# Rows' low half with an operand in PSUM, row stores and one tile moved in the queues, x rows loaded first, last group stored in pieces

## The chip, the cores and the metric

The kernel runs as one program on one core of a Trainium2 chip. The metric is the device time of one execution in microseconds (us), the median of three runs. TensorE (PE), VectorE (DVE), ScalarE (ACT) and GpSimd (POOL) each work through a list of instructions of their own, in order, and wait for each other on semaphores. SyncE (SP) only issues transfers; they run beside the engines on one hardware queue (q1) that 16 DMA engines serve.

## What is computed

The input x and the context have shape (8, 512, 2048), fp32. The reference, cut to what matters:

```python
# 1. autocorrelation attention, 8 heads of 256 columns, per batch
q = layernorm(x); k = v = context
corr = ifft(fft(q) * conj(fft(k))).real            # along the 512 positions
w, idx = top_k(corr, 12); w = softmax(w)           # per batch, head and column
out = sum_i w_i * v[min(idx_i + pos, 511)]
x = x + out
# 2. a linear layer with 16 low-rank updates, on h = layernorm(x)
x = x + h @ W.T + bias + sum_e ((h @ A_e.T) @ Bf_e.T) * (coeffs * scales)_e
```

## The kernel before

The work is written as one pipeline of 78 windows (`for w in range(windows + 1)`, the same loop on each engine's list); a window handles several jobs at once, each at its own delay.

**Attention.** One chunk is one batch and one head: 512 positions by 256 columns. Chunk n has its correlation and its top 12 in window n, its output in window n + 1; there are 64. The transforms are fp32 matmuls with constant matrices, among them `fold` (used first by `values(0)`), which PE can't start without. On POOL, `fold_values` and `fold_queries` add and subtract halves of the operands, `add_products`, `add_upper` and `add_lower` combine products (the helper `add`, line 1042). On DVE, `multiply_queries`, `multiply_upper` and `multiply_lower` multiply PSUM by SBUF (`product`, line 1167). The second half of `multiply_lower` (its tiles a_tw and a_tf) waits until POOL has done the `add_products` of the next window.

**Preparation of the weights, windows 0 to 9.** The 16 row tiles of the combined weight matrix (W plus the low-rank updates) are each made by PE (`delta`, into the PSUM tensor f_ps), added on DVE (`tile_add`), scaled and split into a fp16 high half on ACT (`tile_high`) and a fp16 low half on POOL (`tile_low(n)`, line 1135: p_lo = p_w - p_hi), transposed by DMA (`turn_high`, `turn_low`) and stored to DRAM (`store_high`, `store_low`). Two tiles are done per window. In windows 2 to 9 POOL does `tile_low(2w-4)` after its attention work and `tile_low(2w-3)` at the window's end. So the last tile, number 15, has its low half made at the end of window 9, just ahead of the `add_products` of window 10.

**Rows, from window 9 on.** Row tile r (128 rows, 2048 columns) of batch b is handled in window 9 + 8b + (r mod 4). POOL adds the attention to x (`add_row`), SP stores the sum (`store_x1`), DVE finds the statistics (`row_statistics`, `row_gain`), ACT normalises in place once the store has landed (`row_normalise`, line 959) and writes the fp16 high half row_hi (`row_high`). In the next window, after `multiply_lower`, DVE makes the low half:

```python
def row_low(w, r):
    dve.wait_ge(hi_done, r + 1)
    at_least(dve, h_out, 32 * r)
    nc.vector.tensor_tensor(row_lo[:, :], rows[w % 2][:, :], row_hi[:, :], ALU.subtract).then_inc(lo_done, 1)
```

This is line 1308, tile f_rowlo. Both of its inputs are in SBUF. SP then stores both halves (`store_h`). In window 13 (`LAG - 1`) SP waits until all weights are out, and loads the first weights, and the four row tiles of batch 0 by a transposing DMA (`load_h`, line 516).

**Linear layer, from window 14 on.** Each window runs half of the product of one batch with one group of 512 output columns: 96 fp16 matmuls between the attention's matmuls (high times high, high times low, low times high; lines 781, 783, 785), into f_ps. From there DVE scales (`scale_group`), POOL adds to x1p (`add_group`, 128x512 at a time, four times), and SP stores 1 MB (`store_group`, line 535). There are 32 groups. f_ps is thus free between window 8 and window 14.

**The start.** SP issues chunk 0 of the context (vs) and its last row (last, broadcast to all partitions), the matrix `fold`, four row tiles of x of 1 MB each (`load_first_rows`, line 573, into a_rows and p_w), then chunk 0 of x (xs). DVE finds the first batch's statistics from the four row tiles (`first_statistics`, `first_gain`). ACT's list begins with `double_last(0)`, `move_values(0)`, `move_upper(0)`, which copy PE's results on the context, and only then comes `normalise(0)` (line 875), which needs those statistics. After it POOL begins `fold_queries(0)`.

**Order on SP.** SP's list decides when transfers start, since a wait in it holds back all that stands behind. In window 9 it has `turn_high(14)`, `load_rows`, then the transposes and stores of tile 14 and `turn_high(15)`, and behind them `store_x1(9, 0)` and the load of the next attention rows.

Of the kernel before, what the change touches and what calls it, by code (L numbers as in the profile page):

```python
# [30 lines left out]
ALU = mybir.AluOpType  # L31
# [3 lines left out]
T = 128  # L35
BATCH, L, D = 8, 512, 2048
TB = L // T
# [65 lines left out]
def at_least(engine, sem, value):  # L103

    if isinstance(value, int) and value <= 0:
        return
    engine.wait_ge(sem, value)
# [106 lines left out]
def flow(nc, shared, x, W, A, Bf, coeffs, scales, parts, x1s, hrow, bias, whi, wlo, wscale, out):  # L214
# [12 lines left out]
    with ExitStack() as ctx:  # L227
# [168 lines left out]
        f_shift_done = sem("f_shift_done")  # L396
        h_done = sem("f_h_done")
        hi_done = sem("f_hi_done")
        lo_done = sem("f_lo_done")
        product_mm = sem("f_product_mm")  # L400
        y_done = sem("f_y_done")
# [37 lines left out]
        def _(sp):  # L439
# [23 lines left out]
            def load_attn(r, early):  # L463

                if r >= TILES:
                    return
                at_least(sp, row_added, r)
                if r == 0 and early:
                    sp.wait_ge(delta_mm, TB * OT)
                cols = slice(0, D) if r % TB else slice(0, D - CH) if early else slice(D - CH, D)  # L470
                sp.wait_ge(parts_out, 16 * (CHUNKS * (r // TB + 1) - (r % TB == 0 and early)))
                sp.dma_start(attn[:, cols], part_rows[r * T:(r + 1) * T, cols]).then_inc(attn_in, 16)
# [5 lines left out]
            def store_x1(w, r):  # L478
                sp.wait_ge(row_added, r + 1)
                sp.dma_start(x1s[r * T:(r + 1) * T, :], rows[w % 2][:, :]).then_inc(x1_out, 16)  # L480
# [27 lines left out]
            def load_h(b, q):  # L508

                if b >= BATCH:  # L510
                    return
                unit_read(16 * (b - 1) + 12 + q)
                sp.wait_ge(h_out, 32 * TB * (b + 1))
                cols = slice(q * KQ * T, (q + 1) * KQ * T)
                for dst, part in ((h_hi, 0), (h_lo, 1)):
                    sp.dma_start_transpose(dst[q][:, :, :], hrow[part, b * L:(b + 1) * L, cols]).then_inc(h_in[q], 16)  # L516
# [14 lines left out]

            def store_group(g):
                b, cols = g // 4, slice(g % 4 * WC, (g % 4 + 1) * WC)
                sp.wait_ge(y_added, TB * (g + 1))
                sp.dma_start(out[b, :, cols].rearrange("(i p) d -> p i d", p=T), x1p[:, :, :]).then_inc(out_out, 16)

# [17 lines left out]
            def turn_low(n):  # L554
                sp.wait_ge(p_lo_done, n + 1)
                at_least(sp, p_lo_out, 16 * n)
                sp.dma_start_transpose(p_lo_t[:, :, :], p_lo[n % 2][:, :]).then_inc(p_lo_turned, 16)
# [4 lines left out]
            def store_high(n):  # L562
                sp.wait_ge(p_hi_turned, 16 * (n + 1))
                sp.dma_start(tile_of(whi, n), p_hi_t[n % 2][:, :, :].rearrange("p (q k) o -> p q (k o)", k=KQ)
                             ).then_inc(p_hi_out, 16)

            def store_low(n):
                sp.wait_ge(p_lo_turned, 16 * (n + 1))
                sp.dma_start(tile_of(wlo, n), p_lo_t[:, :, :].rearrange("p (q k) o -> p q (k o)", k=KQ)
                             ).then_inc(p_lo_out, 16)  # L570

            def load_first_rows(k, dst):
                sp.dma_start(dst, x_rows[k * T:(k + 1) * T, :]).then_inc(px_in[k], 16)

            shared.load_v(sp, 0)
            shared.load_fold(sp)
            load_first_rows(0, rows[0][:, :])
            load_first_rows(1, rows[1][:, :])
            load_first_rows(2, w_sb[:, 0, :])
            load_first_rows(3, w_sb[:, 1, :])  # L580
            shared.load_x(sp, 0)
            shared.load_matrices(sp)
            sp.dma_start(ident, shared.consts["ident"]).then_inc(shared.ident_in, 16)
            shared.load_v(sp, 1)
# [15 lines left out]
            for w in range(windows + 1):  # L600
                r, g, at = row_tile(w), finished_group(w), product_window(w)
                made = 1 < w <= PREPARED + 1
                unit = 2 * (w - LAG)
                if 0 < w <= PREPARED:
                    load_rows(w + 1)
                load_x(w + 3)
                if r is not None and r % TB == 0:
                    load_attn(r, False)
                if made:
                    turn_high(2 * w - 4)  # L610
                if at:
                    load_weights(unit + 2)
                if g is not None:
                    store_group(g)
                    load_group(g + 1)
                if row_tile(w - 1) is not None:
                    store_h(row_tile(w - 1))
                if w > PREPARED:
                    load_rows(w + 1)
                if at and at[1] == 7:  # L620
                    for q in range(2):
                        load_h(at[0] + 1, q)
                if made:
                    store_high(2 * w - 4)
                    turn_low(2 * w - 4)
                    load_tile(2 * w - 4 + PW)
                    turn_high(2 * w - 3)
                    store_low(2 * w - 4)
                if r is not None:
                    store_x1(w, r)  # L630
                    if r % TB < TB - 1:
                        load_attn(r + 1, True)
                if w == LAG - 1:
                    sp.wait_ge(p_hi_out, 16 * OT)
                    sp.wait_ge(p_lo_out, 16 * OT)
                    sp.wait_ge(scale_out, 16 * OT)
                    load_weights(0)
                    load_weights(1)
                    load_group(0)
                if at:  # L640
                    load_weights(unit + 3)
                load_v(w + 3)
                if w == LAG - 1:
                    for q in range(4):
                        load_h(0, q)
                if at and at[1] == 7:
                    load_h(at[0] + 1, 2)
                if made:
                    store_high(2 * w - 3)
                    turn_low(2 * w - 3)  # L650
                    load_tile(2 * w - 3 + PW)
                    store_low(2 * w - 3)
                if PREPARED + 1 <= w < PREPARED + 1 + TB:
                    for n in range(TB * (w - PREPARED - 1), TB * (w - PREPARED)):
                        sp.dma_start(wscale[n * T:(n + 1) * T].unsqueeze(1), down[:, n:n + 1]).then_inc(scale_out, 16)
                if 1 <= w <= N:
                    store_parts(w - 1)
                if w >= CHUNKS and w % CHUNKS == 0 and w // CHUNKS <= BATCH:
                    load_attn(TB * (w // CHUNKS - 1), True)
                if at and at[1] == 7:  # L660
                    load_h(at[0] + 1, 3)
            sp.wait_ge(out_out, 16 * 4 * BATCH)

        @block.tensor
        def _(pe):
# [197 lines left out]
        def _(act):  # L863
            def copy(out, source, **how):
                return nc.scalar.activation(out, source, ACT.Copy, **how)  # L865
# [96 lines left out]
            def row_high(w, r):  # L962
                act.wait_ge(h_done, r + 1)
                at_least(act, h_out, 32 * r)
                copy(row_hi[:, :], rows[w % 2][:, :]).then_inc(hi_done, 1)

            def tile_sums(w, n):

# [68 lines left out]
        def _(pool):  # L1037
# [105 lines left out]
            for w in range(windows + 1):  # L1143
                r, g, at = row_tile(w), finished_group(w), product_window(w)
                if 0 < w < N:
                    add_products(w)
                if g is not None:
                    add_group(g)
                if 1 <= w <= N:
                    add_upper(w - 1)  # L1150
                if 1 <= w <= N:
                    add_lower(w - 1)
                if r is not None:
                    add_row(w, r)
                if 1 < w <= PREPARED + 1:
                    tile_low(2 * w - 4)
                fold_queries(w + 2)
                fold_values(w + 2)
                if 1 < w <= PREPARED + 1:
                    tile_low(2 * w - 3)  # L1160
                if at and at[1] % 2 == 1:
                    add_bias(4 * at[0] + at[1] // 2)

        @block.vector
        def _(dve):
# [139 lines left out]
            def row_low(w, r):  # L1305
                dve.wait_ge(hi_done, r + 1)
                at_least(dve, h_out, 32 * r)
                nc.vector.tensor_tensor(row_lo[:, :], rows[w % 2][:, :], row_hi[:, :], ALU.subtract).then_inc(lo_done, 1)  # L1308

            def scale_group(g):  # L1310

# [146 lines left out]
```

## Time and profile before

| | |
|---|---|
| median of 3 runs | 2785.59 us (2785.28 to 2786.66) |
| the profiled execution's own time | 2788.0 us |
| its span, first to last instruction | 2786.0 us |
| PE busy | 2647.7 us, 95% |
| POOL busy | 2165.1 us, 78% |
| DVE busy | 1839.6 us, 66% |
| ACT busy | 1097.0 us, 39% |
| granted TensorE clock, mean | 0.979 |

The profile is of one execution. The engines' busy times overlap. A row of the timeline gives the start, the duration, engine, line and tiles of an instruction (or of several merged ones, x2, x4), and in brackets how long the engine sat idle before it and for what. The chain of waits is followed back from the last instruction; what isn't on it had room. SPq is SP's queue issuing transfers. All rows on which the prediction rests are listed below, in groups.

### The profile page before, as it was taken

The numbers are of one execution on the slowest core, as the hardware profiler recorded it, in microseconds if no ns is written. First come the engines' busy times: TensorE is split into PE (matmuls) and PEld (weight loads), VectorE is DVE, ScalarE is ACT, GpSimd is POOL, SyncE is SP. The second block draws the span as 40 slices with busy tenths as digits, with TensorE's granted clock in tenths as the row PEclk, the third lists the DMA queues.
The fourth block names the chain that finished last, engine by engine and source line by source line (L and its number), as shares of the span: only waits on it lengthen the run. The fifth ranks groups of instructions, "written<-read, shape, count | busy, mean of one in ns | idle before, by whom it ended". The sixth has DMA issues, their size and how long they took to land.

```text
span 2786.0 us, 39716 instructions
## 1 busy us (share of the span) xinstructions
PE 2647.7 (95%) x14112; PEld 1706.3 (61%) x14112; DVE 1839.6 (66%) x4710; ACT 1097.0 (39%) x1873; POOL 2165.1 (78%) x1558
## 2 busy tenths in 40 slices
PE   5999855899999999999999999999999999999998
PEld 4666644566666666666666666666666666664443
DVE  5888889766776677666776677667766577644200
ACT  4777734533343343433444344443433244211000
POOL 5899988777897799877897799877897789645222
PEclk8999978899999999999999999999999999999999
DMA  8499985845676566945776476845775476548953
GB/s 311 113 267 263 247 233 130 239 145 203 234 235 207 192 225 224 262 138 189 248 236 211 174 245 221 248 154 186 249 207 166 168 246 225 165 147 303 293 171 113
DMA packets 444390, 587.30 MB, mean 211 GB/s; under 512 B 216992, under 2 KB 343072, under 8 KB 426528
## 3 DMA queue, kind: packets, MB, share of 16 engines
q1 hardware_dynamic: 444192, 584.76, 66.1%
q8 instruction: 112, 1.84, 0.3%
q14 instruction: 86, 0.70, 0.1%
HBM read 383.35 MB, written 151.00 MB: 192 GB/s over the span
## 4 chain that ended last, share of the span: by engine, by line
PE 79%; POOL 6%; DMA 5%; DVE 5%; SPq 2%; issue 2%; ACT 1%; POOLq 0%; DVEq 0%; ACTq 0%
PE f_ps L781 14%; PE f_ps L785 14%; PE f_ps L783 14%; PE a_ps L710 10%; PE a_ps L668 10%; PE a_ps L746 7%; PE a_ps L761 3%; PE a_ps L762 3%; PE a_ps L723 2%; DVE f_rowlo L1308 2%; POOL p_lo L1135 1%; DMA p_hi_t<-p_hi 1%; SPq L516 1%; DMA out_dram<-f_x1p 1%; DMA x_scratch<-a_rows 1%
## 5 line engine op out<-in xcount | busy, mean ns | idle before, releaser
L781 PE MATMUL f_ps<-f_whi,f_hhi 128*128 128x512 f16 x2048 | 776.9, 379 | 3.9 <-DMA f_hlo<-h_scratch 2.4
L785 PE MATMUL f_ps<-f_whi,f_hlo 128*128 128x512 f16 x2048 | 776.9, 379 | 0.0
L783 PE MATMUL f_ps<-f_wlo,f_hhi 128*128 128x512 f16 x2048 | 776.7, 379 | 0.0
L865 ACT ACTIVATE a_side<-a_ps 128x256 f32<-128x256 f32 (+1 forms) x192 | 87.1, 454 | 961.4 <-PE a_ps L746 726.9
L710 PE MATMUL a_ps<-a_w_lag,lags 128*128 128x256 f16 x3072 | 356.2, 273 | 1.3 <-DVE a_tf L1167 1.3
L785 PEld LDWEIGHTS f_ps<-f_whi,f_hlo 128*128 128x128 f16 x2048 | 200.5, 98 | 242.1 <-issue 0.8
L783 PEld LDWEIGHTS f_ps<-f_wlo,f_hhi 128*128 128x128 f16 x2048 | 200.5, 98 | 224.8 <-issue 0.8
L710 PEld LDWEIGHTS a_ps<-a_w_lag,lags 128*128 128x128 f16 x3072 | 300.2, 98 | 60.2 <-issue 4.6
L781 PEld LDWEIGHTS f_ps<-f_whi,f_hhi 128*128 128x128 f16 x2048 | 200.5, 98 | 212.5 <-issue 5.0
L1042 POOL TENSOR_TENSOR a_prod<-a_prod,a_tf 128x512 f32<-128x512 f32 x128 | 160.5, 1275 | 215.5 <-DVE a_tf L1167 215.5
L1042 POOL TENSOR_TENSOR a_zv<-a_zv,a_tw 128x512 f32<-128x512 f32 x128 | 187.1, 1480 | 132.8 <-DVE a_tf L1167 132.7
L746 PE MATMUL a_ps<-inv,a_prod 128*128 128x256 f32 x1024 | 238.8, 387 | 23.4 <-POOL a_prod L1042 23.4
L1042 POOL TENSOR_TENSOR f_x1p<-f_x1p,f_y 128x512 f32<-128x512 f32 x128 | 160.5, 1287 | 102.5 <-DVE f_y L1167 102.5
L746 PEld LDWEIGHTS a_ps<-inv,a_prod 128*128 128x128 f32 x1024 | 198.1, 194 | 62.3 <-POOL a_prod L1042 28.6
L1167 DVE TENSOR_TENSOR f_y<-f_ps,f_scale 128x512 f32<-128x512 f32 x128 | 81.1, 686 | 198.9 <-PE f_ps L785 171.7
L1042 POOL TENSOR_TENSOR f_x1p<-f_x1p,f_bias 128x2048 f32<-128x2048 f32 x32 | 147.3, 4602 | 70.4 <-DMA f_x1p<-x_scratch 70.4
L668 PE MATMUL a_ps<-a_tv,fold 128*128 128x256 f32 x512 | 133.6, 408 | 54.9 <-ACT a_vk L865 54.9
L1042 POOL TENSOR_TENSOR a_zu<-a_zu,a_tu 128x512 f32<-128x512 f32 x128 | 172.4, 1369 | 4.2 <-DVE a_tu L1167 4.2
L1214 DVE TENSOR_TENSOR a_ps<-a_ps,a_side 128x256 f32<-128x256 f32 x128 | 55.2, 431 | 181.0 <-ACT a_side L865 181.0
L865 ACT ACTIVATE a_w_lag<-a_ps 128x1024 f16<-128x1024 f16 x128 | 124.0, 1020 | 128.2 <-PE a_ps L723 128.2
L1042 POOL TENSOR_TENSOR a_rows<-a_rows,f_attn 128x2048 f32<-128x2048 f32 x32 | 144.2, 4507 | 33.8 <-DMA f_attn<-parts_scratch 33.8
L1167 DVE TENSOR_TENSOR a_prod<-a_ps,a_vk 128x512 f32<-128x512 f32 x128 | 87.9, 687 | 122.3 <-PE a_ps L668 122.3
(130 smaller groups left out, 5324.8 us busy)
## 6 DMA issues: line engine op xcount, KB each, us to landing
f_whi<-whi_scratch SPq DMA_DIRECT2D x128, 512.0 KB, 5.4
f_wlo<-wlo_scratch SPq DMA_DIRECT2D x128, 512.0 KB, 6.6
a_rows<-in_x_dram SPq DMA_DIRECT2D x62, 1024.0 KB, 8.4
vs<-in_ctx_dram SPq DMA_DIRECT2D x64, 512.0 KB, 7.6
xs<-in_x_dram SPq DMA_DIRECT2D x64, 512.0 KB, 3.6
parts_scratch<-a_so SPq DMA_DIRECT2D x64, 512.0 KB, 4.7
x_scratch<-a_rows SPq DMA_DIRECT2D x32, 1024.0 KB, 5.1
f_x1p<-x_scratch SPq DMA_DIRECT2D x32, 1024.0 KB, 6.2
```

What stands on the lines that cost most here:

```text
L668: return nc.tensor.matmul(ps[:, pair, j, :], fold[:, k, :], source, start=True, stop=True)
L710: mm = nc.tensor.matmul(ps[:, pair + k, cls, :], lag_mat[:, constant, j, 2 * cls + k, :], w_lag[:, part, 2 * h + j::TB, :], start=(j == 0 ...
L723: mm = nc.tensor.transpose(turned[:, i * T:(i + 1) * T], w_row[:, part, i // TB, i % TB * T:(i % TB + 1) * T], shared.ident16[:, :])
L746: mm = nc.tensor.matmul(corr[:, g, cls * 2 * T:(cls + 1) * 2 * T], prod[:, 2 * k + cls, g * T:(g + 1) * T], inv[:, cls, k, :], start=(k == ...
L761: nc.tensor.matmul(ps[:, 2 + j, i, :], outm[:, k0, :], z[:, s0, :], start=True, stop=False)
L762: mm = nc.tensor.matmul(ps[:, 2 + j, i, :], outm[:, k1, :], z[:, s1, :], start=False, stop=True)
L781: nc.tensor.matmul(f_ps[:, t, :], h_hi[q][:, kq, rows_t], w_hi[u % WR][:, :, kq, :], start=(k == 0), stop=False)
L783: nc.tensor.matmul(f_ps[:, t, :], h_hi[q][:, kq, rows_t], w_lo[u % WR][:, :, kq, :], start=False, stop=False)
L785: mm = nc.tensor.matmul(f_ps[:, t, :], h_lo[q][:, kq, rows_t], w_hi[u % WR][:, :, kq, :], start=False, stop=(k == DB - 1))
L865: return nc.scalar.activation(out, source, ACT.Copy, **how)
L1042: return nc.gpsimd.tensor_tensor(whole, whole, part, op)
L1167: return nc.vector.tensor_tensor(out, a, b, ALU.mult)
```

## The change

Four edits, and nothing else:

1. For the first four rows (r < 4), ACT copies row_hi once more, as fp32 into the PSUM tensor f_ps, and DVE subtracts that copy instead of row_hi. The result is the same number.
2. On SP, `store_x1` and the load of the next attention rows stand ahead of the tile's transposes and stores. Both are in one window only in window 9.
3. The low half of tile 15 and its transpose and store are taken from window 9 to window 10. On POOL it comes after `add_row` and before `fold_queries`.
4. At the start the first two row tiles of x come first, and `fold` after chunk 0 of x. At the end the last group is stored in four pieces of 256 KB, each after its own addition.

```diff
             def store_group(g):
                 b, cols = g // 4, slice(g % 4 * WC, (g % 4 + 1) * WC)
+                if g == 4 * BATCH - 1:
+                    for t in range(TB):
+                        sp.wait_ge(y_added, TB * g + t + 1)
+                        sp.dma_start(out[b, t * T:(t + 1) * T, cols], x1p[:, t, :]).then_inc(out_out, 16)
+                    return
...
-            shared.load_v(sp, 0)
-            shared.load_fold(sp)
             load_first_rows(0, rows[0][:, :])
             load_first_rows(1, rows[1][:, :])
+            shared.load_v(sp, 0)
             load_first_rows(2, w_sb[:, 0, :])
             load_first_rows(3, w_sb[:, 1, :])
             shared.load_x(sp, 0)
+            shared.load_fold(sp)
...
+                if r is not None:
+                    store_x1(w, r)
+                    if r % TB < TB - 1:
+                        load_attn(r + 1, True)
                 if made:
                     store_high(2 * w - 4)
                     turn_low(2 * w - 4)
                     load_tile(2 * w - 4 + PW)
                     turn_high(2 * w - 3)
                     store_low(2 * w - 4)
-                if r is not None:
-                    store_x1(w, r)
-                    if r % TB < TB - 1:
-                        load_attn(r + 1, True)
...
                 if made:
                     store_high(2 * w - 3)
+                if 1 < w <= PREPARED:
                     turn_low(2 * w - 3)
                     load_tile(2 * w - 3 + PW)
                     store_low(2 * w - 3)
+                if w == PREPARED + 2:
+                    turn_low(OT - 1)
+                    store_low(OT - 1)
...
                 copy(row_hi[:, :], rows[w % 2][:, :]).then_inc(hi_done, 1)
+                if r < TB:
+                    act.wait_ge(hi_done, r + 1)
+                    at_least(act, lo_done, r)
+                    copy(f_ps[:, :, :].rearrange("p a c -> p (a c)"), row_hi[:, :]).then_inc(hi_copied, 1)
...
                 if r is not None:
                     add_row(w, r)
+                if w == PREPARED + 2:
+                    tile_low(OT - 1)
                 if 1 < w <= PREPARED + 1:
                     tile_low(2 * w - 4)
                 fold_queries(w + 2)
                 fold_values(w + 2)
-                if 1 < w <= PREPARED + 1:
+                if 1 < w <= PREPARED:
                     tile_low(2 * w - 3)
...
-                nc.vector.tensor_tensor(row_lo[:, :], rows[w % 2][:, :], row_hi[:, :], ALU.subtract).then_inc(lo_done, 1)
+                high = row_hi[:, :]
+                if r < TB:
+                    dve.wait_ge(hi_copied, r + 1)
+                    high = f_ps[:, :, :].rearrange("p a c -> p (a c)")
+                nc.vector.tensor_tensor(row_lo[:, :], rows[w % 2][:, :], high, ALU.subtract).then_inc(lo_done, 1)
```

## Rows read from the trace of the kernel before

**Rows 1.** Windows: length, busy time of each engine, granted clock, DMA share, GB/s.
```profile
385.50:403.20 17.70, 5.89 (x20) 4.54 (x18) 17.70 (x3) 0.77 (x2) 17.62 (x12) 0.69 0.75 119
625.20:2455.00 1829.80, 1829.80 (x10152) 1204.05 (x10152) 1268.91 (x3290) 713.34 (x1293) 1532.41 (x1118) 1.00 0.64 209
```
**Rows 2.** Timeline of DVE, windows 9 to 13: two waits for POOL, and the four row_low.
```profile
383.09 1.29 DVE L1167 TENSOR_TENSOR a_tw<-a_ps,a_vk 128x512 f32<-128x512 f32 x2 [7.87 <-POOL a_prod L1042]
385.49 17.68 DVE L1308 TENSOR_TENSOR f_rowlo<-a_rows,f_rowhi 128x2048 f16<-128x2048 f32 x1
432.28 2.28 DVE L1308 TENSOR_TENSOR f_rowlo<-a_rows,f_rowhi 128x2048 f16<-128x2048 f32 x1
446.98 2.47 DVE L1290 BATCH_NORM_STATS2 f_bn<-a_rows 128x6 f32<-128x512 f32 x4 [0.79 <-POOL a_rows L1042]
463.48 17.69 DVE L1308 TENSOR_TENSOR f_rowlo<-a_rows,f_rowhi 128x2048 f16<-128x2048 f32 x1
510.52 2.28 DVE L1308 TENSOR_TENSOR f_rowlo<-a_rows,f_rowhi 128x2048 f16<-128x2048 f32 x1
```
**Rows 3.** Chain of waits, windows 9 to 14: start, length, what.
```profile
385.58 17.60 DVE f_rowlo L1308
...
535.28 0.38 PE f_ps L781
```
**Rows 4.** Timeline of POOL over the same windows.
```profile
364.94 1.27 POOL L1071 TENSOR_TENSOR a_tq<-xs 128x512 f32<-128x512 f32 x1
376.47 4.07 POOL L1135 TENSOR_TENSOR p_lo<-p_w,p_hi 128x2048 f16<-128x2048 f32 x1
380.50 2.49 POOL L1042 TENSOR_TENSOR a_prod<-a_prod,a_tf 128x512 f32<-128x512 f32 x2
398.55 1.25 POOL L1071 TENSOR_TENSOR a_tq<-xs 128x512 f32<-128x512 f32 x1
401.10 3.20 POOL L1076 TENSOR_TENSOR xs<-a_tq 128x512 f32<-128x512 f32 x1
425.27 2.52 POOL L1042 TENSOR_TENSOR a_prod<-a_prod,a_tf 128x512 f32<-128x512 f32 x2 [6.84 <-DVE a_tf L1167]
432.44 4.46 POOL L1042 TENSOR_TENSOR a_zv<-a_zv,a_tw 128x512 f32<-128x512 f32 x2 [1.51 <-DVE a_tf L1167]
458.47 2.50 POOL L1042 TENSOR_TENSOR a_prod<-a_prod,a_tf 128x512 f32<-128x512 f32 x2
```
**Rows 5.** DVE groups with an input in PSUM: durations in ns, least, median, most.
```profile
L1256 DVE SCALAR_TENSOR_TENSOR a_w_row<-a_ps,a_sums,a_w_row x128: 740/747/753, 55.4 to 2469.7; 128x512 f16<-128x512 f32 x128
L1167 DVE TENSOR_TENSOR a_zv<-a_ps,a_vk x128: 680/681/692, 69.9 to 2483.6; 128x512 f32<-128x512 f32 x128
L1343 DVE TENSOR_SCALAR p_bt<-f_ps,p_mix x2: 3685/3688/3690, 38.0 to 56.7; 128x2048 f32<-128x2048 f32 x2
```
**Rows 6.** Timeline of ACT around the row work of windows 9 and 10.
```profile
378.11 2.09 ACT L959 ACTIVATE a_rows<-a_rows,f_shift,f_gain 128x2048 f32<-128x2048 f32 x1 [12.51 <-DMA x_scratch<-a_rows]
424.90 1.91 ACT L865 ACTIVATE f_rowhi<-a_rows 128x2048 f16<-128x2048 f32 x1
```
**Rows 7.** Timeline of the start: PE, ACT, the issue of chunk 0 of x.
```profile
4.45 0.64 SPq L179 DMA_DIRECT2D xs<-in_x_dram  x1
14.24 3.75 PE L668 MATMUL a_ps<-vs,fold 128*128 128x256 f32 x8 [14.24 <-POOL vs L1062]
21.34 0.62 ACT L865 ACTIVATE a_uk<-a_ps 128x256 f32<-128x256 f32 x2
23.90 2.07 ACT L875 ACTIVATE xs<-xs,stat 128x256 f32<-128x256 f32 x4 [1.94 <-DVE stat L1336]
```
**Rows 8.** Time to landing of that transfer of chunk 0 of x.
```profile
DMA to landing us min/median/max: 14.7/14.7/14.7
```
**Rows 9.** The last store: its issue in the timeline, its bytes in a window.
```profile
2781.45 0.39 SPq L535 DMA_DIRECT2D out_dram<-f_x1p  x1
2784.00:2785.00 1.00, 0.00 (x0) 0.00 (x0) 0.00 (x0) 0.00 (x0) 0.00 (x0) 0.50 1.02 377
```

More of the change, by code:

```diff
@@ L398, in flow @@
         hi_done = sem("f_hi_done")
+        hi_copied = sem("f_hi_copied")
         lo_done = sem("f_lo_done")
@@ L661, in _ @@
                     load_h(at[0] + 1, 3)
-            sp.wait_ge(out_out, 16 * 4 * BATCH)
+            sp.wait_ge(out_out, 16 * (4 * BATCH - 1 + TB))
         @block.tensor
```

## The prediction

> **What bounds the kernel now.** I read the windows first. From 625 to 2455 us PE is busy for 1829.8 of 1829.8 us at the full clock [rows 1]: in the steady part nothing but PE's own work counts, and the change takes none of it away. What can move is what lies before the first product (it starts at 535.28 [rows 3], when the first transposed low half has landed) and what lies after the last. So I read the chain of waits before 535 next. Its two longest pieces by far are one and the same DVE instruction, the subtraction of line 1308, with 17.60 us each; the first stands in [rows 3]. The timeline shows that the same instruction on the same shape takes 2.28 us in the windows between [rows 2]. Over the first of the two, POOL is busy for 17.62 of 17.70 us, and PE and ACT nearly idle [rows 1]. The held instruction ends at 403.2, and in the last 2 us of it POOL's instruction at 401.10 is stretched to 3.20 us, where its like before it takes 1.25 [rows 4]: DVE gets in there, and holds POOL in turn. In the two short cases it is POOL that had just been waiting 1.5 us for DVE's a_tf, so DVE comes first, and POOL's next pair is stretched [rows 4]. So this is DVE shut out by a row of POOL instructions, when both of its inputs are in SBUF. Before that, window 9 has 7.87 us in which DVE waits for POOL's a_prod, behind tile 15's low half [rows 2, 4].
>
> **Edit 1, the operand in PSUM.** DVE's instructions with one input in PSUM and one in SBUF show no such case: 128 of line 1167 between 680 and 692 ns, 128 of line 1256, with an fp16 input and output, between 740 and 753 ns, in all windows and beside the same POOL work [rows 5]. So I take the hold as gone. The new instruction's own length isn't in the trace. Its ends are 2.28 us (the SBUF form [rows 2]) and 3.69 us (the 2048 columns of line 1343 out of the same f_ps, written with a stride [rows 5]); I take 2.4, since four 512-column products at 0.6 us from start to start come to that, and they are its nearest kin. Each hold is 17.69 - 2.28 = 15.4 us.
>
> ACT gets one copy more per row, 1.91 us by its twin [rows 6], at most 2.1 by line 959 [rows 6]; into PSUM it could be a little shorter, below which I have no row. In window 10 row_hi was done at 424.90 + 1.91 = 426.8, and DVE wanted it at 432.28 [rows 2, 6]: 5.5 us of room for a copy of 1.9, so the new wait costs nothing. Behind it stand `normalise` of a later chunk, which POOL needs a window later, and in window 13 the statistics and `part_corr`: about 1 us there, hidden under the wait for the transposed rows. Were that cover gone, it would be 1 us once.
>
> The Trainium skill (SBUF — State Buffer, "Who interferes with whom") says that a DVE instruction with two SBUF inputs contends with a GpSimd instruction that reads SBUF, and one with at most one SBUF input doesn't; the rows on PSUM inputs agree. Its section "SBUF: two separate sides" has whoever starts first hold the ports for one whole instruction. By that the held DVE would wait for one POOL instruction, 4.5 us at most, and the gain would be 9 us for two, not 31; here the row shows 15.4 us over eleven POOL instructions, and I go by the row.
>
> **Edits 2 and 3, windows 9 and 10.** Without tile 15's 4.07 us, a_prod of window 10 starts at 376.5, not 380.5 [rows 4], and DVE's a_tw 4.0 earlier, at 379.1. ACT doesn't stand in the way: its row_normalise waited 12.51 us for the row's store [rows 6], which SP issued behind the transposes; with the store ahead of them it lands around 366, and row_hi and its copy are done by 374.5. The transposes and stores of tiles 14 and 15 come later on SP by two issues, about 1 us, and nobody waits for them before window 13. So the first row_low starts at 381.5 and ends at 383.9, where before it ended at 403.2: 19.3 us. What DVE does next needs the correlation, which begins with the same a_prod and moves by 4.0 only; it may cost DVE 1 us of this.
>
> In window 10 POOL is now late. From a_prod (380.50) to the first a_tq (398.55) it took 18.05 us, and from a_tq to the next a_prod 11.53 (364.94 to 376.47) [rows 4]. With tile 15 between them: 376.5 + 18.05 + 4.05 + 11.53 = 410.1, a_prod done at 412.6, while DVE would be ready at about 411. So the second row_low starts at 412.7 + 2.4 = 415.1, not 432.28: 17.2 us gained. This is where the moved tile costs its 4 us, of which about 2.4 are covered by DVE's longer window.
>
> From there each window is DVE's: the free one lasted 31.20 us from row_low to row_low (432.28 to 463.48 [rows 2]). Of these 0.79 went on a wait for POOL's row sum [rows 2], which POOL, no longer stretched and waiting (1.51 + 1.96 us at 432.44 [rows 4]), now has ready; plus 0.2 for the longer subtraction: 30.6. POOL's own round is 18.05 + 11.53 = 29.6, just below. So the third starts at 445.7 (before: 463.48) and the fourth at 476.3 (before: 510.52), 34.2 earlier, and ends 34.0 earlier. What follows to the first product, 22.5 us of SP issues and transfers, stays. PE is ready for it with about 2 us of room. Gain by edits 1 to 3: 34.0 us. The ends: 37 if the windows fall to POOL's 29.6, 27 if each subtraction takes 3.69 and POOL holds windows at 33.2 (425.27 to 458.47 [rows 4]).
>
> **Edit 4, start and end.** Up to chunk 0 of x, eight transfers are issued, and in the change the same eight, with `fold` the last instead of chunk 0 of x. The last of the eight landed at 4.45 + 14.7 = 19.1 [rows 7, 8]; so `fold` lands then. PE's first matmul, at 14.24 before [rows 7], needs it: 4.9 us later. ACT copies PE's results before it may normalise; these copies ended at 22.0 [rows 7], now at 26.9, and the statistics, 0.6 earlier than before (256 KB less ahead of the rows), wait for ACT. So normalise(0) starts at 26.9, not 23.90 [rows 7]: 3.0 us lost, and the chain runs from it through POOL without room. The bounds: a gain of 0.6 if `fold` comes in time after all, a loss of 5.
>
> At the end 1 MB is issued at 2781.45, moves at 377 GB/s [rows 9], 2.7 us, and the span ends at 2786.0. Now 256 KB remain after the last addition, 0.7 us: 1.9 us gained (0 to 2.7: the transfer's fixed part stays). The three earlier issues lie under POOL's additions.
>
> The Trainium skill (DMA: Bandwidth & Descriptors, "HWDGE ordering") has descriptors consumed in ring order on each DMA engine. If several transfers shared the bandwidth instead, `fold` would be in before the rows and the start would cost nothing.
>
> **Sum.** -34.0 + 3.0 - 1.9 = -32.9 us. The profiled execution took 2788.0 us, 2.0 more than its span and 2.4 more than the median. So 2755.1 for such an execution, and 2785.6 - 32.9 = 2752.7 for the median.
>
> **Rivals.** (a) POOL becomes the bound between windows 10 and 13: its round is 29.6 against DVE's 30.6, so little is wanting. At 33.2 us a window, and the long form of the subtraction, 27 instead of 34: 2760. For it: its round has hardly a pause. Against: part of the 33.2 was the stretching by row_low. (b) Only one of the two holds goes, or both by half, as they would if the lock were passed on at each instruction: 15.4 less, 2768; by the page's lock rule it is 2775. Against: two holds of the same 17.6. (c) The change doesn't do what it says: the copy in PSUM doesn't free DVE. Then row 0 waits as before for POOL's pause, which the moved tile puts at the same moment, and what remains is +3.0 - 1.9: 2787. (d) Slower: the PSUM form is held as well, and POOL, now less often behind DVE, is in full run at rows 1 and 3 too, which were let through only thanks to its 1.5 us of waiting. Place: row_low of windows 11 and 13; price 15.4 each; one of them is enough: 2787 + 15.4 = 2802. Rows 5 speak against (c) and (d): 256 cases without one.
>
> **Chances.** Forecast 0.78, (a) 0.10, (b) 0.05, (c) 0.04, (d) 0.03. The range 2745 to 2766 takes the forecast with its bounds and (a). This kernel can be told from no change at about 0.2%, 5.6 us. Faster 0.93 (forecast, a, b), same 0.04 (c), slower 0.03 (d).
>
> **What would show it.** Right: f_rowlo at 2.3 to 2.5 us in all four rows; the first product near 504; a_tw's wait for a_prod in window 9 down from 7.9 to about 3.9 us; PE's first matmul at about 19 and ACT's normalise at about 27; some 2 us less between the last addition and the end; the rest of the same length. Wrong: any f_rowlo of the first four over 5 us; ACT as the last releaser of row_low; a product start later than 512.

## The result, and the profile after

Four runs of the changed kernel had a median of 2753.39 us (2749.87 to 2755.55), four of the kernel before beside them 2785.44 us (2783.86 to 2786.66): a ratio of 0.9881, 95% interval 0.9866 to 0.9896. Forecast were 2752.7 us. The profiled execution took 2753.61 us against 2788.0, which is 34.4 us less; the sum had said 32.9.

The page after, its span, the busy times and the shares of the chain by engine:
```profile
span 2751.5 us, 39727 instructions
PE 2642.9 (96%) x14112; PEld 1702.8 (62%) x14112; DVE 1811.5 (66%) x4710; ACT 1103.7 (40%) x1877; POOL 2157.1 (78%) x1558
PE 81%; POOL 6%; DMA 5%; DVE 4%; SPq 2%; issue 2%; ACT 1%; POOLq 0%; DVEq 0%; ACTq 0%
```
The first four row_low are one group now, and ACT has four copies more. The groups by form (duration in ns least, median, most; first to last start; the shapes):
```profile
L1328 DVE TENSOR_TENSOR f_rowlo<-a_rows,f_ps x4: 2274/2277/2278, 381.9 to 477.5; 128x2048 f16<-128x2048 f32 x4
L875 ACT ACTIVATE f_ps<-f_rowhi x4: 1882/1882/1882, 373.7 to 472.1; 128x2048 f32<-128x2048 f16 x4
```
Where two of the four took 17.7 us [rows 2], all four take 2.28. The timeline of DVE in windows 9 to 13, the lines that answer to [rows 2]:
```profile
379.52 1.29 DVE L1183 TENSOR_TENSOR a_tw<-a_ps,a_vk 128x512 f32<-128x512 f32 x2 [2.66 <-POOL a_prod L1056]
381.92 2.28 DVE L1328 TENSOR_TENSOR f_rowlo<-a_rows,f_ps 128x2048 f16<-128x2048 f32 x1
413.19 1.29 DVE L1183 TENSOR_TENSOR a_tw<-a_ps,a_vk 128x512 f32<-128x512 f32 x2 [2.34 <-POOL a_prod L1056]
415.59 2.28 DVE L1328 TENSOR_TENSOR f_rowlo<-a_rows,f_ps 128x2048 f16<-128x2048 f32 x1
419.61 0.43 DVE L1230 TENSOR_TENSOR a_ps<-a_ps,a_side 128x256 f32<-128x256 f32 x1 [1.07 <-ACT a_side L875]
447.44 2.27 DVE L1328 TENSOR_TENSOR f_rowlo<-a_rows,f_ps 128x2048 f16<-128x2048 f32 x1
477.51 2.28 DVE L1328 TENSOR_TENSOR f_rowlo<-a_rows,f_ps 128x2048 f16<-128x2048 f32 x1
```
The wait for a_prod ahead of the first is down from 7.87 to 2.66 us; there is now a short wait for POOL in the next window as well (2.34). The same stretch on POOL, where [rows 4] has its lines of before:
```profile
376.93 2.49 POOL L1056 TENSOR_TENSOR a_prod<-a_prod,a_tf 128x512 f32<-128x512 f32 x2
...
382.51 2.49 POOL L1056 TENSOR_TENSOR a_zv<-a_zv,a_tw 128x512 f32<-128x512 f32 x2
...
395.01 4.06 POOL L1149 TENSOR_TENSOR p_lo<-p_w,p_hi 128x2048 f16<-128x2048 f32 x1
...
401.61 1.27 POOL L1090 TENSOR_TENSOR xs<-a_tq 128x512 f32<-128x512 f32 x1
...
410.59 2.49 POOL L1056 TENSOR_TENSOR a_prod<-a_prod,a_tf 128x512 f32<-128x512 f32 x2
```
Nothing of POOL is stretched in these windows any more: the pair of additions at 382.51, beside the first row_low, takes 2.49 us, where [rows 4] shows 4.46 for such a pair, and the instruction at 401.61 takes 1.27, where [rows 4] shows 3.20 for its like. DVE and POOL run past each other. Tile 15 stands where it was moved to, at 395.01.

The first product, from the timeline of PE:
```profile
502.26 0.38 PE L791 MATMUL f_ps<-f_whi,f_hhi 128*128 128x512 f16 x1 [1.57 <-DMA f_hlo<-h_scratch]
```
It stood at 535.28 [rows 3], so 33.0 us come from ahead of it. From there to the start of DVE's four products of the last group (`scale_group`) it is 2240.1 us before and 2240.4 after. That they agree so closely says little: over the ten traces of this document this stretch lies between 2237.8 (the second trace of the changed kernel) and 2240.5, with no order by kernel, so it is unchanged within some 2.7 us. From those products to the end of POOL's last addition it is 6.05 us in both. From there to the end of the span 4.6 us have become 2.8. 33.0 - 0.3 + 1.8 = 34.5, which is the whole difference of the spans.

### The profile page after: what moved, and what is told of

Its sections match the earlier page's. It is cut to its first block, busy times and chain, and to the rows that moved or that the text cites. A ratio compares the mean times of both kernels' runs of the same rounds, so it can differ in the third digit from the quotient of the medians.

```text
span 2751.5 us, 39727 instructions
## 1 busy us (share of the span) xinstructions
PE 2642.9 (96%) x14112; PEld 1702.8 (62%) x14112; DVE 1811.5 (66%) x4710; ACT 1103.7 (40%) x1877; POOL 2157.1 (78%) x1558
## 4 chain that ended last, share of the span: by engine, by line
PE 81%; POOL 6%; DMA 5%; DVE 4%; SPq 2%; issue 2%; ACT 1%; POOLq 0%; DVEq 0%; ACTq 0%
PE f_ps L791 15%; PE f_ps L793 15%; PE f_ps L795 15%; PE a_ps L678 10%; PE a_ps L720 10%; PE a_ps L756 7%; PE a_ps L771 3%; PE a_ps L772 3%; PE a_ps L733 2%; POOL p_lo L1149 1%; SPq L517 1%; PE f_ps L817 1%; DMA out_dram<-f_x1p 1%; DMA x_scratch<-a_rows 1%; DMA p_hi_t<-p_hi 1%
## 5 line engine op out<-in xcount | busy, mean ns | idle before, releaser
L1056 POOL TENSOR_TENSOR a_zf<-a_zf,a_tf 128x512 f32<-128x512 f32 x128 | 159.4, 1264 | 0.0
```

The lines of the kernel that those rows point to most:

```text
L1056: return nc.gpsimd.tensor_tensor(whole, whole, part, op)
```

## The experiments

Two sets, each on one chip beside the kernel before: the first four rows of the table (there the kernel before had a median of 2786.52 us), and the last four (2786.99 us). "Row_low" gives the start of the four, with the length where it isn't 2.28 us.

| kernel | median us | ratio, 95% interval | row_low of rows 0 to 3, us | first product |
|---|---|---|---|---|
| edit 1 alone | 2754.3 | 0.9889, 0.9874 to 0.9903 | 383.3, 414.0, 445.3, 475.3 | 500.39 |
| edits 2 and 3 alone | 2787.7 | 1.0002, 0.9993 to 1.0011 | 382.6 (21.7), 432.0, 463.2 (17.7), 510.2 | 535.93 |
| all, operand in SBUF | 2787.6 | 1.0004, 0.9994 to 1.0013 | 379.8 (21.7), 431.1, 462.5 (17.5), 509.6 | 534.86 |
| PSUM for rows 0 and 2 | 2768.3 | 0.9943, 0.9927 to 0.9960 | 384.8, 418.4 (17.7), 463.8, 493.9 | 518.75 |
| the change again | 2754.4 | 0.9884, 0.9869 to 0.9898 | 381.4, 415.1, 445.8, 477.1 | 502.19 |
| old start | 2752.3 | 0.9873, 0.9858 to 0.9887 | 380.0, 413.6, 446.1, 477.4 | 503.19 |
| before, with one wait | 2758.5 | 0.9896, 0.9882 to 0.9911 | 385.9 (2.8), 417.6 (2.8), 449.2 (2.8), 481.6 | 507.48 |
| with two moves more | 2747.4 | 0.9860, 0.9843 to 0.9876 | 377.9, 409.7, 439.7, 471.1 | 496.66 |

**Edit 1 alone.** The kernel before with this, and nothing moved:
```diff
+                if r < TB:
+                    act.wait_ge(hi_done, r + 1)
+                    at_least(act, lo_done, r)
+                    copy(f_ps[:, :, :].rearrange("p a c -> p (a c)"), row_hi[:, :]).then_inc(hi_copied, 1)
...
+                    high = f_ps[:, :, :].rearrange("p a c -> p (a c)")
+                nc.vector.tensor_tensor(row_lo[:, :], rows[w % 2][:, :], high, ALU.subtract).then_inc(lo_done, 1)
```


> Edit 1 alone on the kernel before. Theory (two SBUF inputs let POOL shut DVE out): f_rowlo of the first four rows at 2.3 us each, the first product near 503.5 (535.3 less 31.7: window 9 keeps its 4 us of tile 15, window 10 loses nothing to it), no gain at the end: 2756 in the profiled execution, about 2754 median, ratio 0.9886. Rival (the queue edits carry a good part): at most half of the gain, 2770 or more.

Its timeline of DVE:
```profile
380.86 1.29 DVE L1172 TENSOR_TENSOR a_tw<-a_ps,a_vk 128x512 f32<-128x512 f32 x2 [6.39 <-POOL a_prod L1047]
383.26 2.28 DVE L1317 TENSOR_TENSOR f_rowlo<-a_rows,f_ps 128x2048 f16<-128x2048 f32 x1
...
475.32 2.29 DVE L1317 TENSOR_TENSOR f_rowlo<-a_rows,f_ps 128x2048 f16<-128x2048 f32 x1
```
Its ratio can't be told from that of the whole change: edit 1 is the gain. What edits 2 and 3 add is seen when the times are counted from one point that both kernels pass alike, the low half of tile 13 in window 8. From there to the four row_low it is 47.4, 78.1, 109.4 and 139.4 us here, and 43.7, 77.3, 109.2 and 139.2 in the change: a start 3.7 us ahead at the first, of which 0.8 is left at the second and 0.2 at the fourth. Tile 15's 4 us of POOL only went from window 9 to window 10.

**Edits 2 and 3 alone**, with row_low out of SBUF:

> Edits 2 and 3 alone, row_low with two SBUF inputs. Theory: the first row_low starts 4 us earlier and is still held until POOL's first pause, which the tile moved into window 10 keeps at about 403; from there all is as before: 2788 +-1.5, ratio 1.000. Rival (the queue edits give their 4 us for themselves): 2784 or less. Second rival (POOL in full run holds rows 1 or 3 as well): 2803 or more.

DVE's row 0, then POOL's list beside it:
```profile
382.60 21.68 DVE L1315 TENSOR_TENSOR f_rowlo<-a_rows,f_rowhi 128x2048 f16<-128x2048 f32 x1
```
```profile
395.65 4.04 POOL L1140 TENSOR_TENSOR p_lo<-p_w,p_hi 128x2048 f16<-128x2048 f32 x1
...
402.21 3.20 POOL L1081 TENSOR_TENSOR xs<-a_tq 128x512 f32<-128x512 f32 x1
```
The subtraction is 4.0 us longer than 17.68 [rows 2], which is the length of the one instruction put into POOL's list. So the hold lasts as long as the list, and by itself the move brings nothing that the times show.

**All of the change, the operand in SBUF.** The copy, its wait and its place stay; DVE reads the other operand:
```diff
                 high = row_hi[:, :]
                 if r < TB:
                     dve.wait_ge(hi_copied, r + 1)
-                    high = f_ps[:, :, :].rearrange("p a c -> p (a c)")
```


> The changed kernel, with the copy into PSUM and the wait for it kept, but DVE subtracting row_hi from SBUF. Theory: rows 0 and 2 are held 15 us or more each, row 1 is let through; first product near 535, 2786.5 profiled, ratio 1.000. Rival (it is the later start or the order of waits that frees DVE, not the operand): f_rowlo near 2.3 us, 2753.6, ratio 0.988.

DVE's timeline of it, row 0:
```profile
379.82 21.66 DVE L1327 TENSOR_TENSOR f_rowlo<-a_rows,f_rowhi 128x2048 f16<-128x2048 f32 x1
```
This differs from the change in one operand only and loses all of it. So neither ACT's copy nor the wait for it, which shifts when DVE asks, makes the gain; the operand does. It differs in two ways, though: it lies in SBUF and is fp16, where the copy lies in PSUM and is fp32. No run has an fp32 copy in SBUF. That the memory decides and not the type is argued: line 1256 reads an fp16 operand in SBUF beside one in PSUM and was never held [rows 5], so an fp16 operand alone doesn't make the hold; but no held or free instruction with two fp32 inputs in SBUF was measured.

**PSUM for rows 0 and 2 only**, the two that were held before. Here the theory and rival (d) differ: is a row that was let through still let through when POOL no longer waits ahead of it?
```diff
-                if r < TB:
+                if r in (0, 2):
```


> The changed kernel with the PSUM operand for rows 0 and 2 only; rows 1 and 3 subtract from SBUF. Theory (what decides is whether POOL is in full run when DVE asks): in the changed kernel row 1 asks at 415.6, between two POOL instructions without a pause until 431; so row 1 is held, 15 to 16 us, and row 3, which asks while POOL waits for DVE's a_tf, is not: one window more, 2768 profiled, ratio 0.994. Rival (the holds belong to rows 0 and 2, by their buffer or place): no f_rowlo over 3 us, 2753.6, ratio 0.988.

DVE's row 1, and POOL from before it asks until it is let in:
```profile
418.38 17.67 DVE L1328 TENSOR_TENSOR f_rowlo<-a_rows,f_rowhi 128x2048 f16<-128x2048 f32 x1
```
```profile
418.30 0.71 POOL L1056 TENSOR_TENSOR a_zu<-a_zu,last 1x256 f32<-1x256 f32 x1
...
432.64 1.25 POOL L1086 TENSOR_TENSOR a_tq<-xs 128x512 f32<-128x512 f32 x1
433.97 3.20 POOL L1090 TENSOR_TENSOR xs<-a_tq 128x512 f32<-128x512 f32 x1
...
494.02 4.46 POOL L1056 TENSOR_TENSOR a_zv<-a_zv,a_tw 128x512 f32<-128x512 f32 x2 [0.38 <-DVE a_tf L1183]
```
Row 1, free in the kernel before, is held for 17.67 us here, and half of the gain is gone. Row 3 is free again: POOL had waited 0.38 us just before. So which rows are held isn't a matter of the row but of whether POOL's list has a pause when DVE asks. That part of rival (d) is real; it doesn't touch the change because all four rows read PSUM.

Where DVE is let in can be read from the code: the stretched instruction is the same in each held row (401.10 [rows 4], 402.21 and 433.97 above), and it is the one ahead of which `fold_queries` waits for POOL's own instruction just before (`pool.wait_ge(q_halved, n + 1)`). The next run puts a wait of this kind where DVE asks.

**One wait for POOL.** The kernel before, in which POOL waits ahead of the additions into a_zv for its own addition just before:
```diff
                 pool.wait_ge(w0_used, 2 * (n + 1))
+                pool.wait_ge(zu_raised, n + 1)
                 add(zv[:, 0:2, :], tw[:, 0:2, :], ALU.add)
```


> The kernel before with one wait more on POOL: ahead of add_lower's first addition it waits for its own last instruction, so that its list has a pause just where DVE asks for row_low. Nothing else. Theory (DVE gets in at POOL's first pause, however short): f_rowlo of rows 0 and 2 at about 3 us instead of 17.7, each window loses 2.3 us of POOL in turn, first product near 507, 2759.5 profiled, ratio 0.990. Rival (a pause of this kind is too short, or DVE waits its turn over a number of instructions): still 15 us or more for rows 0 and 2, ratio 1.000.

DVE's row 0, and POOL beside it:
```profile
385.89 2.78 DVE L1309 TENSOR_TENSOR f_rowlo<-a_rows,f_rowhi 128x2048 f16<-128x2048 f32 x1
```
```profile
385.80 0.71 POOL L1042 TENSOR_TENSOR a_zu<-a_zu,last 1x256 f32<-1x256 f32 x1
386.65 4.37 POOL L1042 TENSOR_TENSOR a_zv<-a_zv,a_tw 128x512 f32<-128x512 f32 x2
```
Both operands are in SBUF, and the row takes 2.78 us. POOL stood still from 386.51 to 386.65; that 0.14 us is enough to let DVE in. The price is on POOL: its pair takes 4.37 us, not 2.49, 1.9 in each window with a row_low. From tile 13's low half the first row_low comes after 47.4 us, as with edit 1 alone, and the fourth after 143.1, which is 3.7 more; POOL lost three times 1.9 in between, of which 2.0 don't show in DVE's times. In the whole time this kernel and edit 1 alone can't be told apart by their intervals.

**The change again, with old start, and with two moves more.** "Old start" has the loads of the start in their old order and is otherwise the change. The last kernel has the old start too; the low half of tile 15 is made by DVE in window 9, out of a copy in PSUM as the rows are; and of the last group, the third and fourth row tile are multiplied and added by DVE, with the product left in PSUM:
```diff
+                    dve.wait_ge(last_copied, 1)
+                    nc.vector.tensor_tensor(p_lo[(OT - 1) % 2][:, :], w_sb[:, (OT - 1) % PW, :],
+                                            f_ps[:, :, :].rearrange("p a c -> p (a c)"), ALU.subtract
+                                            ).then_inc(last_low, 1)
...
+                    if g == 4 * BATCH - 1 and t >= 2:
+                        product(f_ps[:, t, :], f_ps[:, t, :], scale_sb[:, :]).then_inc(y_in_ps, 1)
+                        nc.vector.tensor_tensor(x1p[:, t, :], x1p[:, t, :], f_ps[:, t, :], ALU.add
+                                                ).then_inc(half_added, 1)
```


> The changed kernel once more, on the same chip as the three that follow, as what they are compared with: ratio 0.988, about 2753.

> The changed kernel with the start's transfers in the old order. Theory of the prediction (fold last costs the start): PE's first matmul back at 14.2 and ACT's normalise at 23.9 instead of 25.5, and if nothing takes it up on the way, 1.6 us off the whole, 2751.8. What the two traces suggest instead: the transfer-paced windows 3 to 8 swallow it (the delay was 1.55 us at POOL's first fold_queries and 0.3 us at tile 13's low half in window 8), so the whole stays within 1 us of the changed kernel.

> A version meant to beat both: the changed kernel with the old start, tile 15's low half made on DVE in window 9 with its high half in PSUM (instead of on POOL in window 10), and in the last group the additions of the third and fourth row tile on DVE, out of PSUM. Theory: DVE's wait for a_prod in window 10 (2.34 us) goes, the last addition ends 2 us sooner; 2749 profiled, ratio 0.9865. Rival (transfers or ACT take it back): no better than the changed kernel, 0.988.

With the old start ACT's first `normalise` begins at 23.58 us, with the new one at 25.47 and 26.15. The whole is 2.1 us shorter, but the intervals overlap. Tile 13's low half, ahead of which all kernels do the same but for the start, begins between 334.4 and 339.3 us in six traces with the old start, the kernel before among them, and between 336.3 and 341.3 in four with the new. The means are 1.4 us apart, within spreads of 5. There is one more comparison: the kernel with the operand in SBUF has the new start and the last store in pieces, the one with edits 2 and 3 alone has neither (nor ACT's copies). The last store in pieces is worth 1.8 us, yet their medians, of ten runs each on one chip, differ by 0.2 (2787.6 and 2787.7), which leaves 1.6 for the new start. None of these is clear of the spread by itself; all of them point to a cost of 1.4 to 2.1 us, where the expectation for the old start's run had leaned to under 1. So the new start probably costs something, but that isn't shown.

DVE's timeline of the last kernel:
```profile
343.38 2.28 DVE L1433 TENSOR_TENSOR p_lo<-p_w,f_ps 128x2048 f16<-128x2048 f32 x1
...
407.25 1.28 DVE L1195 TENSOR_TENSOR a_tw<-a_ps,a_vk 128x512 f32<-128x512 f32 x2
...
2740.48 0.69 DVE L1352 TENSOR_TENSOR f_x1p<-f_x1p,f_ps 128x512 f32<-128x512 f32 x1
```
The tile takes DVE 2.28 us instead of POOL's 4.06, and the wait of 2.34 us ahead of a_tw is gone. From tile 13's low half to the fourth row_low it is 136.7 us, where the change has 139.2 in both of its traces and the kernel with the old start, which does the same there, 140.9: 2.5 to 4.2 gained. At the end, from DVE's first product of the last group to the end of the span, 8.8 us have become 7.6. It is the shortest of all kernels here: 0.9860 of the kernel before; against the change's 0.9884 the intervals overlap a little.

## Why the prediction was right

**The hold and its end.** Taken: two holds of 15.4 us, gone with the operand in PSUM. Measured: all four at 2.28 us, and with row_hi in SBUF as the operand the loss of everything. The mechanism is as stated, and stronger than stated: the hold follows POOL's list to the instruction (17.7 us; 21.7 with 4.04 more in the list; 2.8 with a pause of 0.14). The rule in the Trainium skill (SBUF — State Buffer, "SBUF: two separate sides"), that whoever starts first keeps the ports for one whole instruction, gives a wait of less than 5 us here. The runs show eleven instructions of POOL in a row, twelve with the tile, and the measurement decides. The same page's "Who interferes with whom", that a DVE instruction with at most one SBUF input doesn't contend, agrees with all runs here. One reading of the prediction was loose: over the first hold PE was busy for 5.89 of 17.70 us [rows 1], which isn't "nearly idle"; nothing was worked out from it.

**Length of the new subtraction.** Taken 2.4 us, between 2.28 and 3.69; it is 2.28, the length of the SBUF form. The ACT copy, taken at 1.91, is 1.88, and it was never what row_low waited for.

**Windows 9 and 10.** The wait for a_prod was to fall to 3.9 us; it is 2.66 in one trace and 3.71 in the second (there at 379.03), so the forecast holds about as well as two executions agree. The second row_low was foretold at 415.1 and measured at 415.59; POOL's a_prod done at 412.6, measured 413.08. That is where POOL is late, and the moved tile costs there what the step said: of the lead of 3.7 us at the first row, which edits 2 and 3 gave, 0.8 is left at the second.

**The free windows.** Taken 30.6 us each; measured 31.85 and 30.07, and 30.74 and 31.26 in the second trace. They follow from one number: a window lasts 30.1 us, and what DVE waits for ACT's copies of PE's results comes on top. In the 31.85 these are two waits, 1.07 us for the correlation's odd half (419.61, above) and 0.65 for the output's; in the 30.07 there is none; in the second trace 0.69 (30.74) and 1.12 (31.26). This stretch of PE, first its timeline, then the window's totals (busy time by engine, granted clock, DMA share, GB/s), shows what was late ahead of the first of the two:
```profile
413.14 6.02 PE L756 MATMUL a_ps<-inv,a_prod 128*128 128x256 f32 x16 [4.22 <-POOL a_prod L1056]
```
```profile
413.00:419.20 6.20, 6.06 (x17) 4.95 (x18) 5.35 (x7) 0.39 (x2) 6.20 (x7) 0.61 1.20 46
```
PE had waited 4.22 us for POOL. The granted clock over the stretch was 0.61, so it was for the most part at the lower of its two levels (1.2 GHz), and the sixteen matmuls took 6.02 us, where a window later, at 443.04 and a clock of 1.00, they took 3.68. The second wait, on DVE, and PE ahead of it:
```profile
427.97 1.19 PE L771 MATMUL a_ps<-a_zu,outm 128*128 128x256 f32 x2 [1.13 <-issue]
434.06 0.69 DVE L1299 TENSOR_TENSOR a_so<-a_ps,a_side 128x512 f32<-128x512 f32 x1 [0.65 <-ACT a_side L875]
```
From 427.90 to 431.50 the granted clock was 0.50, the lower level; a window later the same two matmuls took 0.67 us at a clock of 1.00, and DVE didn't wait. That DVE might have to wait for the correlation was in the working for the first row ("it may cost DVE 1 us of this"), but not for the later ones; nor was PE's clock. All in all the fourth row_low comes 33.0 us earlier, where 34.2 were foretold before the shift of the start; rival (a), POOL at 33.2 us a window, didn't come about.

**The start.** The landing of `fold` was foretold for 19.1 and measured at 18.8 us, 14.0 after its issue, where in the old order it landed after 6.0: it did wait behind what was issued ahead of it. But `normalise` started at 25.47 (26.15 in the second trace), not at 26.9. The term of 3.0 us was mis-sized: it moved the whole chain of PE by the delay. The chain in the change, the transfer's issue, the wait for the context's last row on ACT, POOL's last work on the context, PE and ACT:
```profile
4.76 1.26 SPq L187 DMA_DIRECT2D fold<-const_fold_dram  x1
11.67 1.28 ACT L875 ACT_TABLE_LOAD   x1 [11.67 <-DMA last<-in_ctx_dram]
17.44 1.27 POOL L1076 TENSOR_TENSOR vs<-a_tv 128x512 f32<-128x512 f32 x1
18.86 3.46 PE L678 MATMUL a_ps<-vs,fold 128*128 128x256 f32 x8 [18.86 <-POOL vs L1076]
22.15 1.03 PE L678 MATMUL a_ps<-a_tv,fold 128*128 128x256 f32 x4
23.40 1.13 PE L678 MATMUL a_ps<-a_tv,fold 128*128 128x256 f32 x4 [0.22 <-ACT a_vk L875]
24.94 0.62 ACT L875 ACTIVATE a_uk<-a_ps 128x256 f32<-128x256 f32 x2
25.47 2.06 ACT L885 ACTIVATE xs<-xs,stat 128x256 f32<-128x256 f32 x4
```
PE starts 4.6 us later than at 14.24 [rows 7], where 4.9 were said. That this came out so near has an element of luck, since the prediction named one path and there are two. PE's weight loads waited for `fold` until 18.83, but POOL's work on the context ended only at 18.71, where it ended at 14.1 before: with two row tiles of x ahead of it, the context's last row reached ACT at 11.67 instead of 7.07. By these rows PE would still have started at about 18.7 with `fold` in time, and the gain of 0.6, one of the bounds, wasn't to be had in this order. ACT's last copies start only 3.6 us later than at 21.34 (4.3 in the second trace): the second set of eight matmuls took 2.4 us from 22.15 on, 3.1 before. ACT had stood idle for 1.94 us ahead of `normalise` for the statistics [rows 7], and nothing of that is left; the local loss is 1.6 us (2.2 in the second trace). At window 8 the first trace and that of the kernel before are 0.3 us apart, which says little beside the spread given above.

**The end.** Taken -1.9, measured -1.8 us. The first three issues of 256 KB lie beside the additions; the additions end at 2748.73, the issues at 2749.09, the span at 2751.5. POOL's timeline and SP's:
```profile
2743.80 4.93 POOL L1056 TENSOR_TENSOR f_x1p<-f_x1p,f_y 128x512 f32<-128x512 f32 x4 [19.89 <-DVE f_y L1183]
```
```profile
2745.10 3.99 SPq L538 DMA_DIRECT2D out_dram<-f_x1p  x4
```

**The sum.** -33.0 for the first product with the start in it, +0.3 for the stretch after, -1.8 for the end: -34.5. Foretold were -34.0 + 3.0 - 1.9 = -32.9. From tile 13's low half to the first product the gain was 33.3 us where 34.0 were said, the stretch after gave 0.3 and the end 0.1 less, and up to tile 13 only 0.3 of the 3.0 said were lost; that is the 1.6 us between the sums. This adds up for one pair of traces. Since tile 13 alone moves by 5 us between traces of one start, and the stretch after the first product by 2.7, that the total came within 1.6 us (and the median within 0.7) is in part luck: the middle gained less than said and the start cost less than said, and the two offset each other in part. What isn't luck is the two holds, 31 of the 34 us of the middle: they went as described, in every trace with the operand in PSUM.

## What to carry to other kernels

A DVE instruction with both inputs in SBUF that takes many times its length in some executions and not in others, while GpSimd's list beside it has no gap, is shut out and not slow: look at the longest instances of a group rather than at its mean, and at what GpSimd does over them. Putting one of its two SBUF inputs in PSUM cures it without taking anything from GpSimd, and a copy by an idle engine pays for that; where no PSUM is free, one pause in GpSimd's list where the DVE instruction asks gives most of the gain (28.5 of 32.6 us by the medians). Moving GpSimd's work about only moves the hold, and every row that is "let through" in the old kernel is so by luck of timing: cure at once all of its kind that lie on the chain of waits. The 28 later row tiles still subtract out of SBUF here, in 2.28 to 5.11 us, at most 2.8 us over the free length, and 24 of them where PE is busy throughout.

## What the runs showed that was not expected

- POOL's instructions follow each other without a gap (starts 2.45 us apart for lengths of 2.49). The held DVE instruction gets in at the first seam: in the run with rows 0 and 2 this is before 433.97, where POOL stood for 0.08 us after the one at 432.64 ended; a forced pause of 0.14 us does it too. The steps between instructions that don't wait for the one just before show no such pause.
- The same kernel isn't the same in every execution near the end of a batch: at the last batch's first products PE waited 2.4 us in all for weights in one trace of the change and 0.2 in the other. The waits of PE after 2500 us (total, times, longest), first one trace, then the other:
```profile
PE f_ps L791 <- DMA f_wlo<-wlo_scratch: 2.4, 2, 1.3
```
```profile
PE f_ps L791 <- DMA f_wlo<-wlo_scratch: 0.2, 1, 0.2
```
That difference of 2.2 us lies between the 1.6 that the new start lost locally and the 3.0 that it was to cost, one reason more why the start couldn't be settled by whole times.
